# A two-layer transformer program on one core: three small reorderings in the loop of the first layer

## The reference, cut to what matters

```
xn = layernorm(x)
x  = x + attention(xn) + experts(xn)

attention: q = rope(xn @ W_q);  lat = layernorm(xn @ W_dkv);  k = rope(lat @ W_uk);  v = lat @ W_uv
           16 heads of 8 features, causal softmax(q k^T) v, then @ W_o
experts:   4 of 32 experts of width 64 per token (silu(x g) * (x u)) @ d, weighted, plus a shared expert of width 128
```

## Time and profile before

| | |
|---|---|
| median of 3 runs | 2765.76 us (2764.23 to 2774.04) |
| the profiled execution, its own time | 2770.14 us |
| its span, first to last instruction | 2768.3 us |
| first loop, from the first ScalarE step of pass 0 to the last sum L1477 | 68.9 to 1053.6 us of the span |
| mean granted TensorE clock | 0.915 |
| busy share of the span: PE, DVE, ACT, POOL | 89%, 73%, 41%, 11% |
| chain that ended last: PE, DVE, issue | 56%, 25%, 12% |

### The profile page before, as it was taken

One profiled execution on the slowest core, in us unless ns is written; L12 is line 12 of the kernel. 1 busy time (PEld: TensorE's weight loads), 2 busy tenths in 40 slices (PEclk: granted clock), 3 DMA queues, 4 the chain that ended last, 5 costly groups with the idle time before them and its releaser, 6 DMA issues.

```text
span 2768.3 us, 48745 instructions
## 1 busy us (share of the span) xinstructions
PE 2453.1 (89%) x15408; PEld 1596.9 (58%) x15408; DVE 2028.8 (73%) x6361; ACT 1136.2 (41%) x2066; POOL 311.6 (11%) x236
## 2 busy tenths in 40 slices
PE   2989888898989887899899899899899899899898
PEld 1434344443444444586586586586586586577576
DVE  4857676685867777768777867867867966966976
ACT  0132322313232234446446445445445445544544
POOL 1000000000000001121121110210210211211211
PEclk8988889898988987999999999999899999899999
DMA  5230413212130312201201201101101101211210
GB/s 157 78 93 24 108 37 88 55 62 72 46 103 25 105 43 66 69 5 58 70 4 59 62 9 62 54 17 62 47 25 62 47 25 36 66 32 32 62 39 31
DMA packets 158271, 152.01 MB, mean 55 GB/s; under 512 B 81128, under 2 KB 122672, under 8 KB 157520
## 3 DMA queue, kind: packets, MB, share of 16 engines
q1 hardware_dynamic: 155024, 142.83, 18.0%
q10 hardware_dynamic: 3008, 6.36, 0.6%
HBM read 121.29 MB, written 27.85 MB: 54 GB/s over the span
## 4 chain that ended last, share of the span: by engine, by line
PE 56%; DVE 25%; issue 12%; ACT 3%; DMA 2%; POOL 1%; SPq 1%; DVEq 0%; ACTq 0%; POOLq 0%
PE bank L910 5%; PE bank L922 5%; PE bank L580 4%; PE bank L592 4%; PE bank L583 4%; PE bank L608 3%; PE bank L502 3%; DVE arena L1605 3%; DVE arena L1663 3%; DVE arena L1661 3%; PE bank L648 3%; PE bank L897 2%; PE bank L879 2%; DVE arena L1617 2%; PE bank L870 2%
## 5 line engine op out<-in xcount | busy, mean ns | idle before, releaser
L922 PEld LDWEIGHTS bank<-wring,arena 128*128 128x128 f32 x2048 | 279.9, 202 | 136.4 <-issue 99.0
L1166 ACT ACTIVATE arena<-bank,w_b 128x512 f32<-128x512 f32 x256 | 175.1, 687 | 369.6 <-PE bank L910 369.3
L910 PE MATMUL bank<-arena,wring 128*128 128x512 f32 x512 | 295.0, 662 | 30.9 <-ACT arena L1166 30.9
L922 PE MATMUL bank<-wring,arena 128*128 128x128 f32 x2048 | 284.7, 287 | 22.8 <-DVE arena L1778 15.2
L1605 DVE SCALAR_TENSOR_TENSOR arena<-bank,w_convw,arena 128x511 f32<-128x511 f32 (+2 forms) x384 | 254.9, 737 | 11.6 <-ACT arena L1076 11.6
L1045 ACT ACTIVATE arena<-bank 128x512 f32<-128x512 f32 (+1 forms) x384 | 172.5, 534 | 186.9 <-PE bank L635 185.3
L1449 DVE CUSTOM_DVE_ANT_0 bank<-bank,arena 128x128 f32<-128x128 f32 (+3 forms) x512 | 249.2, 492 | 0.0
L1036 ACT ACTIVATE arena<-bank 128x512 f32<-128x512 f32 x128 | 76.5, 598 | 397.4 <-PE bank L580 397.4
L502 PE MATMUL bank<-w_ident,arena 128*128 128x128 f32 (+2 forms) x652 | 114.9, 303 | 84.5 <-DVE arena L1345 51.9
L592 PE MATMUL bank<-arena 128*128 128x128 f32 x1088 | 157.5, 288 | 2.7 <-DVE arena L1434 2.7
L580 PE MATMUL bank<-arena 128*128 128x512 f32 x256 | 148.7, 664 | 0.0
(11 more groups left out here) (284 smaller groups left out, 4845.8 us busy)
## 6 DMA issues: line engine op xcount, KB each, us to landing
wring<-in_w_last SPq DMA_DIRECT2D x66, 512.0 KB, 3.3
arena<-scrw SPq DMA_DIRECT2D x260, 128.0 KB, 3.0
arena<-scrg SPq DMA_DIRECT2D x32, 512.0 KB, 5.4
arena<-scrq SPq DMA_DIRECT2D x36, 192.0 KB, 3.8
arena<-scrk SPq DMA_DIRECT2D x36, 192.0 KB, 4.5
scrn<-arena SPq DMA_DIRECT2D x64, 64.0 KB, 1.9
arena<-scrn SPq DMA_DIRECT2D x8, 512.0 KB, 3.7
scrx<-arena SPq DMA_DIRECT2D x8, 512.0 KB, 3.5
```

The costliest lines, as they stand in the source:

```text
L910: mm(bank[HBANK[f]][:, :], wring[:, e % 2, k * P:(k + 1) * P], xn1T, start=True, stop=True).then_inc(*s["p_fh"].up)
L922: last = mm(bank[o][:, t * P:(t + 1) * P], GH[:, f % 2, t * P:(t + 1) * P], wring[:, e % 2, FC * P + k * D:FC * P + (k + 1) * D], start=(f ...
L1166: fn(GH[:, f % 2, :], bank[HBANK[f]][:, :], ACT.Gelu_apprx_tanh, bias=W["b1"][:, f:f + 1]).then_inc(*s["a_gh"].up)
```

## The change

It does four things, all in the first loop:

- ScalarE's copy of x to xr is no longer the second instruction of the pass; it becomes a step of its own, `("xr",)`, behind the silu of gate product 2 (the third gate product, counting from 0). The copy of V follows the first silu at once.
- The transposed maxima go into bank 4 instead of bank 0, in both halves. The 33rd block of scores (n = 32) and the fourth score of the second stage no longer wait for the copy of these rows (`v_nmt`), but for the maximum that used the bank before them.
- `fnorm` is cut in two: `fstat` (statistics and variance, up to the semaphore that GpSimd's power waits for) and `fnorm` (the wait for GpSimd and the four normalizations).
- At the end of the first stage the order `maxneg 1, hid 16, wbd 15, maxrows 1, wbd 16, fnorm` becomes `hid 16, fstat, maxneg 1, wbd 15, maxrows 1, wbd 16, fnorm`.

```diff
@@ schedule_l0
-        order += [("gu", p), ("hid", p - 1)] + ([("maxrows", 0)] if n == 32 else [])
+        order += [("gu", p)] + ([("xr",)] if p == 2 else []) + [("hid", p - 1)] + ([("maxrows", 0)] if n == 32 else [])
...
-    order += [("maxneg", 1), ("hid", PR0), ("wbd", PR0 - 1), ("maxrows", 1), ("wbd", PR0), ("fnorm",)]
+    order += [("hid", PR0), ("fstat",), ("maxneg", 1), ("wbd", PR0 - 1), ("maxrows", 1), ("wbd", PR0), ("fnorm",)]
@@ TensorE
-                    bk = after(*(("v_nmt", 1) if n == 32 else ("v_max", max(n - 1, 0))), (0, 2)[n % 2])
+                    bk = after("v_max", max(n - 1, 0), (0, 2)[n % 2])
...
-                    bk = after("v_max", 32 * half + 31, 0)
+                    bk = after(*(("v_nmt", 1) if half else ("v_wt", 1)), 4)
...
-                    last = (("a_sg", PR0 + 1), ("v_max", NH * NT), ("v_hid", PR0 + 1), ("v_nmt", 2))
+                    last = (("a_sg", PR0 + 1), ("v_max", NH * NT), ("v_hid", PR0 + 1), ("v_max", NH * NT))
@@ ScalarE
                 fn(SG[:, 0, :], bank[1][:, :], ACT.Silu).then_inc(*s["a_sg"].up)
-                act.wait_ge(*s["v_x1"].at(b, 0))
-                fn(xr[:, :, :], x[:, :, :], ACT.Copy).then_inc(*s["a_xr"].up)
                 act.wait_ge(*s["p_v"].at(b, 1))
...
+                def residual():
+                    act.wait_ge(*s["v_x1"].at(b, 0))
+                    fn(xr[:, :, :], x[:, :, :], ACT.Copy).then_inc(*s["a_xr"].up)
@@ VectorE
-            def fnorm(b, k):
+            def fstat(b, k):
                 dve.wait_ge(*s["x_in"].at(b, 16 + 16 * k))
                 norm_stats(chain("v_flink", b, k), x, stats, mv, var4[:, :], EPS0).then_inc(*s["v_var"].up)
+
+            def fnorm(b, k):
                 dve.wait_ge(*s["g_rstd"].at(b, 1, k))
...
-                    v.tensor_copy(nmt[rows], bank[0][0:32, 0:P]).then_inc(*s["v_nmt"].up)
+                    v.tensor_copy(nmt[rows], bank[4][0:32, 0:P]).then_inc(*s["v_nmt"].up)
```

More of the change, by code:

```diff
@@ L1481, in dve_steps @@
                 return {"hid": hid, "max": smax, "maxneg": maxneg, "maxrows": maxrows, "pv": pv, "attn_out": attn_out,
-                        "fnorm": later(fnorm), "fq": later(fq), "flat": later(flat), "flatT": later(flatT), "fk": later(fk),
+                        "fstat": later(fstat), "fnorm": later(fnorm), "fq": later(fq), "flat": later(flat), "flatT": later(flatT), "fk": later(fk),
                         "froute": later(froute), "fw": later(fw)}
```

4 lines of the change are left out of this document (2 added, 2 removed).

## The result

The changed kernel took 2757.35 us in the median of 15 runs (2750.57 to 2775.29), the kernel before 2772.61 (2762.01 to 2778.57) beside it: a ratio of **0.9955**, 95% interval 0.9939 to 0.9971, or 12.5 us less. The forecast was 3.4 us less than the kernel before (2762.4 against 2765.8). The ratio, applied to the same 2765.8, gives 2753.3: inside the range of 2749 to 2775, and on the fast side of the forecast. The profiled execution of the changed kernel took 2753.51 us, with a span of 2751.7.

What follows compares the result with a forecast made beforehand. VectorE was taken to set the first stage's pace, with half-clock query products at its end. 2770.1 - 7.7 - 2.0 + 0 + 6.4 = 2766.8; that execution stood 4.4 over the median, so 2762.4 us, range 2749 to 2775.

Steps and rivals of the forecast that it cites:

- the first term: Start of a pass: moving the copy to xr ends VectorE's 1.10 us idle, -7.7 us in 7 passes.
- The bound: First stage: VectorE sets the pace, so its 1.10 us wait at the start lies on the path; TensorE's waits do not.
- The copy, -7.7: Start of a pass: V's copy starts earlier, L583 loses its 1.16 us wait, VectorE its 1.10; bounds 0 and -8.2.
- The rival by which something else would be late: Start of a pass: VectorE's idle 1.10 us would pass to another release; total 2772 us, chance 0.10.
- Falls of the clock in the first stage, -2.0: Start of a pass: most of two clock falls, 1.60 us each, go; bounds -3.2 and 0.
- The bank, 0: First half of the rows: TensorE's 1.26 us wait only shifts, the four falls 35 us in stay; bound -6.4.
- The statistics, +6.4: End of first stage: normalization 0.6 us earlier, but half clock behind a longer gap; +0.8 a pass, between -10 and +14.
- the first rival: End of first stage: clock back before the query products, or no drop before them; total 2746 to 2753, chance 0.17.
- The rule on transposes: End of first stage: matmuls directly behind the gap would raise the clock sooner than transposes, giving a total of 2746 to 2753.
- The second rival: From the gap through the next sample's front: half clock holds, slower than before; +17 us, 2783, chance 0.07.
- The sum: Whole kernel: copy, falls, bank and statistics added to the profiled 2770.1 give 2766.8, median 2762.4 us.

Runs made afterwards that it cites:

- copy and second half: Against the kernel before: copy to xr moved, and only the second half of the rows of maxima in bank 4; 2756.74 us, ratio 0.9937.
- the longer pass: Changed kernel plus a 0.91 us fill of a scratch tile on VectorE before its second expert product; 2764.97 us, ratio 0.9985 to the kernel before.
- the last kernel: Copy moved and statistics ahead, without bank 4, plus unread products in two of TensorE's gaps; 2771.31 us, ratio 1.0007 to the kernel before.

## Why the prediction was right or wrong

The time fell inside the range and to the side that was forecast. Of the mechanism the first term is right. The rest of the 12.5 us came by a way that the sum did not have, and that the total lies within the range is in part the width of the range.

*The bound.* Right: in the first stage VectorE sets the pace, and its wait at the pass's start went in full, once TensorE was there in time.

*The copy, -7.7.* Right: -1.20 us in 7 passes, 8.4. The rival by which something else would be late is out. Nothing was queued badly behind the moved copy: it starts at 316.44 and takes 0.62 us, and the load of x behind it never held up the statistics: VectorE has no wait for it in any of passes 1 to 7.

*Falls of the clock in the first stage, -2.0.* This is the term that was mis-sized: in the traces it is -9.6, all six falls. Of these, -3.2 are the two at the pass's start, the lower bound of this term; -6.4 are the four at 35 us, the lower bound of the bank's term, which was taken as 0. The step that failed is "the passes become shorter and so meet the clock's check elsewhere, and the fall 35 us in may take their place". It did not take their place: without the bank that fall did not come in any of 28 passes behind an x1 with the copy or the statistics changed (copy, statistics, both, copy and second half), and it came in 4 of 7 of the kernel before. The reason given for the two falls at the start, that the wait leaves TensorE less idle, is not shown either: the statistics alone, and bank and statistics, keep that wait of 1.17 us in every pass and have no fall there in passes 1 to 7. That the passes now meet the clock's falls at other places by their length is an argument; the longer pass supports it, and no run isolates it.

*The bank, 0.* Right for VectorE and for the place of TensorE's idle time ("stands idle as long after it"; 1.52 us against 1.26), and wrong to leave the falls as they were. Its worth is not a number of its own: +26 us beside the copy, within the noise beside copy and statistics (0.9955 against 0.9944), +6 alone. In the changed kernel no fall stands near 35 us; in copy and bank it stands in each pass.

*The statistics, +6.4.* Against the trace of before the sign holds and the size is half: from the last maximum to the end of a pass 0.65 us more in passes 1 to 7, 4.5 in all, 3.4 with the first pass. As the worth of this part it does not hold: taken out of the changed kernel, the statistics leave it 11 us slower (copy and bank, 0.9996), because the fall at 35.6 us then comes in every pass, 1.56 us each. How an edit at 62 us into the pass removes a fall at 35 us is not shown. The reason was half right. The gap of 2.29 us (2.8 forecast) went with a drop of the clock ahead of the down product, 1.97 us (2.1 forecast); but the like gap of 2.37 us did so in none of seven passes of the statistics alone and in three of seven of copy and statistics. The transposes of xn began 5.8 us behind the last maximum (5.5 before) and not 7.2: TensorE went on about 0.5 us sooner than forecast, and the scores took 1.5 us (377.82 to 379.34) and not 2.2, since at 379 the clock was up again. The normalization began 1.05 us earlier than before, where 0.66 was forecast. The clock came back before the query products, so the rotation starts 2 us earlier than in most passes before: that is the first rival's mechanism, to which I gave 0.17, and the statistics alone show it in passes 2 to 7, in its other form, with no drop before the query products. But its time did not follow: 0.8 us went back before the routing weights, where half clock now holds 20.5 us and not 17.1, and in three of seven passes 3 us in falls near the end. Neither place was in my sum, although the trace of before had a fall near the end in two passes, 1.7 us each.

*The rule on transposes* (the Trainium skill, "TensorE: Matmul & The Clock Gate", Part 4, that a transpose does not count as TensorE activity the way a matmul does): the order with matmuls directly behind the gap had its clock back before the query products in passes 1 to 7 of the changed kernel, the kernel before, with transposes behind the gap, in none. That agrees with the rule, but there the gap also ends later. Against it stand seven passes of the order with matmuls (two of copy and statistics, two of bank and statistics, three of the longer pass) in which half clock held for 10.2 us behind the gap, longer than the 6.8 at most of the kernel before. So no run here settles it.

*The second rival* (half clock through the chain) did not come in the changed kernel; single passes of three other kernels had it, with half clock for 10 us and 2.4 to 3.4 us more up to the rotation.

*The sum.* -7.7 - 2.0 + 0 + 6.4 = -3.3 was forecast; the traces give -8.4 - 9.6 + 0 + 3.4 + 0.3 = -14.3 in the first loop (the 0.3 is the rounding of these steps and the start of the first pass), -2.3 in the second loop, where no term was. That is the 16.6 between the two profiled executions; by the ratio of all runs the kernel moved by -12.5. The three terms that moved all came out lower than forecast, so nothing cancelled; but the eight combinations show that such a sum is an account of one trace, and does not say what each part is worth.

What stays open: which of the passes gets which fall cannot be worked out from the sum of the edits; the runs show it after the fact. The copy alone has 6 runs, fewer than the others, and its interval only just clears that of the whole change.

## What to carry to other kernels

Idle time of TensorE can cost twice: once if somebody waits, and once more if the clock drops for the work that follows, which may be on the path where the gap was not. So a wait that nobody feels is still worth a look at the granted clock behind it, in every pass and not in one: the same gap had a fall behind it in all passes of one kernel and in none of another. Moving such a wait is not free: beside the moved copy it cost 26 us. Try the parts of a change one at a time; here the copy alone was 0.5% better than the three together, and what the other two were worth depended on what stood beside them.

## What the runs showed of the hardware

**Adding work made a kernel faster.** 1.02 us of products a pass in a gap of 1.52 us took 17 us off 2773, and the clock stayed at 1.00 behind the gap. It does not hold everywhere: filling the gap ahead of the transposes of xn cost 17 us beside the copy alone.

**The same gap, with and without a fall.** 1.52 us idle, 32.4 us into the pass: clock 0.50 at 35.6 us in seven of seven passes of copy and bank, 1.00 in seven of seven of the changed kernel.

**A loop can hold its length.** With the statistics alone a pass took 122.85 to 122.87 us (passes 2 to 6), with copy and bank 122.87 to 122.90, although the second starts its maxima 1.2 us earlier; each of the two has its falls at the same places in each of these passes. What is saved in such a pass comes back as half clock elsewhere in it. The copy alone, with the falls of the first stage gone, broke out of it (119.4 to 121.4). Copy and bank with the gap filled, and the last kernel, hold another length: 119.45 to 119.47 us in passes 2 to 6 of the first, 119.42 to 119.46 in passes 1 to 6 of the second.

**Unedited code moves by more than the change.** The second loop took from 1706 us (copy and statistics) to 1756 (the last kernel) in the profiled runs, with the same instructions. Its passes of 207.6 us (changed kernel) had half clock for 17.1 us, those of 211.7 (before) for 27.3, of 215.3 (changed kernel) for 34.1 and of 218.3 (last kernel) for 44.4: 10.7 us more for 27.3 more at half clock, about 0.4 us for each.
